# A decoder layer on one core: GpSimd centres the context rows right behind their load, and splits the transposed context behind the key stacks

## The reference

```python
def attention(x):                                   # 16 query heads over 4 key heads
    scores = einsum('bshd,bthd->bhst', rope(q), rope(k)) * scale
    return (softmax(scores) @ v).reshape(b, s, HIDDEN) @ Wo

def mlstm(q, k=ctx, v=ctx):                         # causal; q is the normalised attention result
    x = concatenate([q, k, v], axis=-1)
    ig, fg = x @ Wi + bi, x @ Wf + bf
    log_D = masked cumulated log_sigmoid(fg) + ig
    D = exp(log_D - max(log_D))
    C = (q @ k.T) / sqrt(dh) * D
    h = C / (maximum(abs(C.sum(-1)), exp(-max_log_D)) + EPS) @ v
    mu = h.mean(-1); var = ((h - mu) ** 2).mean(-1) # per head, 32 features
    return (h - mu) * rsqrt(var + EPS) * ln_scale

def experts(x):                                     # 2 of 16 experts for each token, and one for all
    ...
x = layernorm(x + attention(x))
x = layernorm(x + mlstm(x, ctx_2048, ctx_2048))
x = layernorm(x + experts(x))
```

## Time and profile before

| | us |
|---|---|
| median of 3 runs | 2085.5 (2080.51 to 2090.78) |
| the profiled execution | 2090.95 |
| its span, first to last instruction | 2089.3 |
| TensorE busy | 1871.2 |
| VectorE busy | 1196.6 |
| GpSimd busy | 696.2 |
| granted TensorE clock, mean | 0.951 |

### The profile page before, as it was taken

One profiled execution on the slowest core, in us unless ns is written; L12 is line 12 of the kernel. 1 busy time (PEld: TensorE's weight loads), 2 busy tenths in 40 slices (PEclk: granted clock), 3 DMA queues, 4 the chain that ended last, 5 costly groups with the idle time before them and its releaser, 6 DMA issues. The chain is left out here.

```text
span 2089.3 us, 35576 instructions
## 1 busy us (share of the span) xinstructions
PE 1871.2 (90%) x11010; PEld 1185.8 (57%) x11011; DVE 1196.6 (57%) x2474; ACT 650.3 (31%) x1358; POOL 696.2 (33%) x754
## 2 busy tenths in 40 slices
PE   3879999999999999999999999998879999999990
PEld 2456575766657576665757666575644444444440
DVE  2567777766776776677777667776442222222225
ACT  1142433334243333424333342433302212222224
POOL 3124133332413333241333324133123444444430
PEclk8789999999999999999999999999979999999995
DMA  7153242344424234441423444142324666656549
GB/s 274 44 124 98 56 118 72 90 110 89 118 42 118 72 88 111 89 118 42 118 72 89 111 89 118 41 99 62 105 102 87 134 168 163 148 121 142 90 77 334
DMA packets 151843, 226.92 MB, mean 109 GB/s; under 512 B 32448, under 2 KB 107200, under 8 KB 149056
## 3 DMA queue, kind: packets, MB, share of 16 engines
q1 hardware_dynamic: 101616, 132.94, 24.6%
q0 software_dynamic: 38336, 92.38, 18.4%
q10 hardware_dynamic: 11792, 0.61, 0.4%
HBM read 94.70 MB, written 48.83 MB: 69 GB/s over the span
## 5 line engine op out<-in xcount | busy, mean ns | idle before, releaser
L1575 PE MATMUL ps<-ug_w,rowsT 128*128 x640 | 292.8, 601 | 8.1 <-SPq L1424 4.5
L1575 PEld LDWEIGHTS ps<-ug_w,rowsT 128*128 128x128 f32 x640 | 123.0, 193 | 163.7 <-issue 163.7
L1464 POOL DMA_INDIRECT sum_rows<-y_sb,pairs x80 | 127.3, 1591 | 248.6 <-DVE y_sb L1542 136.5
L869 DVE RECIPROCAL arden<-ps 128x256 f32<-128x256 f32 x64 | 112.5, 1758 | 140.2 <-PE ps L1321 136.6
L1064 PE MATMUL ps<-wqkv_sb,xT_sb 128*128 128x256 f32 (+1 forms) x512 | 172.3, 490 | 15.3 <-ACT maskr_sb L524 15.3
L1530 DVE SCALAR_TENSOR_TENSOR silu<-tanh,ps 128x256 f32<-128x256 f32 x80 | 33.7, 422 | 251.7 <-ACT tanh L1485 251.7
L961 DVE SCALAR_TENSOR_TENSOR weighted<-ps,decay 128x384 f32<-128x384 f32 x256 | 139.2, 553 | 66.4 <-PE ps L1190 50.4
L851 DVE TENSOR_REDUCE smax<-ps 128x2 f32<-128x512 f32 x256 | 164.0, 682 | 16.5 <-PE ps L1247 16.5
L476 POOL DMA_INDIRECT routed_ids<-pair_w,pos_w x64 | 64.0, 1000 | 324.7 <-DVE pair_w L747 288.1
L641 ACT ACTIVATE probs<-ps 128x1024 f32<-128x1024 f32 x128 | 130.8, 1024 | 114.8 <-PE ps L1298 114.8
L620 ACT ACTIVATE decay<-ps,g_col 128x256 f32<-128x256 f32 x256 | 121.3, 474 | 137.5 <-PE ps L1173 90.8
(11 more groups left out here) (253 smaller groups left out, 3835.0 us busy)
## 6 DMA issues: line engine op xcount, KB each, us to landing
q_stack<-qkT_hi SPq DMA_DIRECT2D x128, 128.0 KB, 3.8
mk_stack<-ctxT_hi SPq DMA_DIRECT2D x128, 128.0 KB, 5.1
mq_stack<-qkT_hi SPq DMA_DIRECT2D x128, 128.0 KB, 2.4
ug_w<-in_expert_ug SPq DMA_DIRECT2D x16, 1024.0 KB, 5.3
xT_sb<-in_xT SPq DMA_DIRECT2D x16, 512.0 KB, 3.3
x_sb<-in_x POOLq DMA_DIRECT2D x16, 512.0 KB, 3.8
ctxT_sb<-in_ctxT POOLq DMA_DIRECT2D x16, 512.0 KB, 3.6
q_stack<-qkT_lo SPq DMA_DIRECT2D x64, 128.0 KB, 4.3
```

The lines of the kernel that those rows point to most:

```text
L1464: pool.indirect_dma_start(out=sum_dram, out_offset=bass.IndirectOffsetOnAxis(ap=tables.pairs[:, m, 0:1], axis=0), in_=y_sb[:, m % W, :], i ...
L1575: ins = nc.tensor.matmul(ps[:, 2 + k % 2, :], rowsT[:, k % 2, c, :], ug_w[:, bass.ds(slot, 1), c, :].rearrange("p o n -> p (o n)"), start= ...
```

## The change

In GpSimd's turn three things move. The centring of the context rows no longer stands at the start of the next turn (`centre(y)`) but in the turn that loads them, right behind that load and ahead of the power of hvar (`centre(b)`). The split of the transposed context, with the load behind it, no longer stands ahead of the key stacks but behind them, ahead of the transfers of the routed pairs. Nothing is added or removed: GpSimd, VectorE, TensorE and the others execute as many instructions as before, with the same operands.

```diff
             def body(b, y, w, more):
-                if y is not None:
-                    centre(y)
-                if b is not None:
+                def split_context():
 
                     wait(pool, ctxT_in, b, 16)
                     if y is not None:
...
                         wait(pool, ctx_lo_done, b, 1, rest=rest)
                         pool.dma_start(ctxT_sb[:, :, :], one(ctxT, b + 1)).then_inc(ctxT_in.sem, 16)
 
+                if b is not None:
                     wait(pool, t_ready, b, 0)
                     wait(pool, qk_lo_done, b, 2, rest=rest)
                     stack(pool, k_stack, qkT_hi, qkT_lo, KC, k_in, K_ROWS)
+                    split_context()
...
                     pool.dma_start(ctx_sb[:, :, :, :].rearrange("p t h d -> p (t h d)"), one(ctx_v, b)).then_inc(ctx_row_in.sem, 16)
+                    centre(b)
                 if y is not None:
                     wait(pool, hvar_done, y, 1)
```

## The result

| | before | changed |
|---|---|---|
| median, us | 2088.14 (4 runs, 2080.51 to 2102.47) | 2150.09 (4 runs, 2143.03 to 2152.03) |
| profiled execution, us (span) | 2090.95 (2089.3) | 2143.03 (2140.8) |
| TensorE busy, us | 1871.2 | 1883.8 |
| mean granted clock | 0.951 | 0.945 |

The changed kernel is slower: 1.0282 of the time before, interval 1.0221 to 1.0344. The forecast was 2137 us, 1.0247.

What follows compares the result with a forecast made beforehand. TensorE, busy 1871.2 of 2089.3 us, was taken to pay in full for VectorE's delays between the averages. 28 + 27 - 3.8 = +51 us on 2090.95 gave 2142, or 2137 us on the median's footing; range 2095 to 2158.

Steps and rivals of the forecast that it cites:

- x1: TensorE's waits for x1 from L880: three of four go and the long one shrinks by 1.3 us, -3.8 us.
- The old split: Ahead of the key stacks: L917 and L918 lose 2.8 us per turn, but L921 stands idle anyway, worth 0.
- The split behind the key stacks: GpSimd's cast and subtract hold L948 and L949; first decay product 2.0 us late in 14 turns, 28 us (0 to 31).
- the cast is let in at 844.62: After the last key stack: GpSimd's split cast runs once VectorE's L945 ends, for 1.04 us, ahead of L948.
- L949 stays at 0.33: Sign of being wrong: VectorE's L949 ahead of the first decay product not stretched to 2 to 2.8 us.
- The rival in which the cast asks too late: Cast asks later than 844.65, L948 and L949 slip through; only the centring costs: 2109 us, chance 0.19.
- The centring: Behind the context rows' load: its long subtract holds VectorE, delaying `average(1)` and pair 6; 27 us (0 to 54).
- I take 1.8 us, the turn above, in 15 turns: Delay of `average(1)` and pair 6 by the moved centring, chosen from 0.9 to 3.6 us per turn: 27 us.
- Cannot miss a stretch of 2.3 us: A 6.3 us centring must meet VectorE's 2.3 us stretch that starts 9.7 us behind the load's issue.
- The power of `hvar`: Behind the moved centring: starts about 888.1, ends 893.6, still covered since L994 is itself 1.8 us late.
- neither: Rival: VectorE is held by neither moved piece, only the gain at x1 is left: 2082 us, chance 0.13.
- Only the split costs: Rival: small instructions take turns smoothly, long subtract let in after L844: 2110 us, chance 0.08.

Runs made afterwards that it cites:

- the experiment: Changed kernel, with the split also waiting until VectorE has written gm_rows: 0.9999 of the time before (0.9978 to 1.0021).

## Why the prediction came out right

The forecast of +51 us on the profiled execution met +51.5 us of span, and slower was forecast with 0.81. It got there by its mechanism, with two errors of size that nearly cancel. The medians are 62 us apart on the first chip and 45 us on the second.

- **x1: -3.8 forecast, -3.8 measured.** The three short waits went and the long one is 3.5 us.
- **The old split: 0 forecast.** L918 and L919 became 2.8 us shorter per turn and no wait of TensorE fell by it. Right.
- **The split behind the key stacks: 28 forecast, 30.8 measured.** The mechanism stands, with the held instructions one place off. The step "the cast is let in at 844.62", behind L945 of before, failed: it took the recorded starts for the order of asking. VectorE's cast was recorded 0.3 us ahead of GpSimd's and was held all the same. So one of the prediction's own signs of being wrong came true, "L949 stays at 0.33": the hold was there, but not on L948 and L949. The cost was at its upper bound (2.2 us a turn), since whichever two are held, the holds fill the same 3.5 us. The rival in which the cast asks too late falls with it; only the wait added in the experiment brought that about.
- **The centring: 27 forecast, 17.8 measured** (10.6 alone, and 19.9 - 6.3 = 13.6 in the changed kernel on another chip). This is the mis-sized term. The step that failed is "I take 1.8 us, the turn above, in 15 turns". One turn had been followed through and taken for all, though the place of VectorE's stretch and of the load's landing (4.7 to 7.6 us in the changed kernel) both move from turn to turn. The extra wait is 1.2 us a turn (17.8 / 15), and none in two turns. "Cannot miss a stretch of 2.3 us" was wrong too: in the turn at 612 us VectorE begins L837 11.95 us behind the load's issue, and the centring is over at 11.01. In the other turn without an extra wait, L845 began 0.07 us ahead of the long subtract. That the small instructions take turns with GpSimd's short pieces, at a small price, was right; they cost pair 6 about 0.4 us a turn on the second chip where the long subtract holds nothing.
- **The power of `hvar`: covered, right.** It starts at 915.45 in the turn shown, behind the subtract, and no wait of TensorE for what follows it appears in the list.
- **PSUM-fed work untouched: right** (L962, and L823 at 0.42 us). The reduce wasn't held either, as the Trainium skill (SBUF — State Buffer, Who interferes with whom) has it: 1220 ns before and changed.
- **The clock: not in the sum, +12.6 us of busy time, 1.7 us of it offset by shorter waits for `weighted`.** It is the missing term. A new wait of 2.2 us in a row of dense products was priced at its length only. Two smaller terms were missing as well, the 2.3 us at decay that the new wait covers and the 2.1 us at the start of the run.

With the centring at 17.8 and no clock, the sum would have been 28 + 17.8 - 3.8 = 42 us. That the total came out to half a microsecond is luck, in the two errors and in which executions were profiled; that the change is slower, and by which two places, was read from the rows. Of the rivals, "neither" falls by the holds in all 14 turns. "Only the split costs" (2110, 0.08) came nearest in kind: the split alone is 1.018 to 1.020, beside a total of 1.021 on the second chip, and the centring alone 1.002. But the price of the split in that rival was too low by the clock, and the centring's waits are there in every trace that has it right behind the load (15.7 to 24.4 us for `sq`); in the centring alone a higher clock hides part of them.

## What to carry to other kernels

Before work is moved on GpSimd, lay it beside what VectorE does in SBUF in the new place, and ask who waits for that: each queued GpSimd instruction can hold one VectorE instruction for all of its length. Where it falls on a chain that TensorE waits for, one wait that moves it behind the last such instruction makes it free, and costs nothing while GpSimd has slack. To price a wait of TensorE in dense work, add the slower products behind it to the wait's own length, and take off what other waits give back. A shorter wait elsewhere is put down to the slower clock only if it comes back when the clock does: a version with the clock kept up told them apart here.

## What the runs showed of the hardware that was not expected

- A VectorE cast recorded from 870.06 was held by a GpSimd cast recorded from 870.38: it ended 0.15 us behind GpSimd's. Undisturbed, at 0.27 us, it would have been over at 870.33. So recorded starts do not tell which engine gets hold of SBUF first. It wasn't the issue of the last key stack, until 870.38, that held it: in the kernel before, the same cast ran beside such an issue (842.33 to 844.35) in its 0.27 us.
- GpSimd and VectorE alternate while both have work queued: cast, subtract, subtract against cast, tensor-scalar, gm_rows, each VectorE instruction ending 0.1 to 0.2 us behind its opposite.
- Holds between short instructions are small, but they are there. Beside GpSimd pieces of 0.24 to 1.3 us, L837 and L839 went from 0.19 to 0.3 to 0.7 us in many turns of the centring alone and of the changed kernel on the second chip, and pair 6 waited about 0.4 us more.
- A wait of 2.2 us let the granted clock fall to 0.67 to 0.84 over the next ten microseconds in most turns, and unread products in the wait kept it at 0.99. The median fell by 4.7 us with overlapping intervals, after 5.6 us for the products themselves.
- With the centring in the back of the turn the mean granted clock was higher than in the kernel before on the same chip (0.950 and 0.9525 against 0.945), and its extra waits showed in the time only in part. Why the clock was higher is not shown.
